# Filtering the sum and the difference of two channel tiles in an attention kernel on TensorE

## What is computed

```python
# x: (16, 256, 32, 32); theta_w, phi_w: (32, 256); g_w: (128, 256); o_w: (256, 128)
theta = einsum('bchw,kc->bkhw', x, theta_w)           # 32 channels, 1024 positions n
phi   = pool2(einsum('bchw,kc->bkhw', x, phi_w))      # 32 channels, 256 positions m
beta  = softmax(einsum('bnk,bkm->bnm', theta, phi))   # over m
g     = pool2(einsum('bchw,kc->bkhw', x, g_w))        # 128 channels, 256 positions
o     = einsum('bchw,kc->bkhw', einsum('bcm,bnm->bcn', g, beta), o_w)
z     = gamma * o + x
out   = z + einsum('fc,bchw->bfhw', tpl, z)   # tpl: circulant 256 x 256, 27 taps wide
```

## Time and profile before

| | us |
|---|---|
| median of 3 runs | 272.98 (272.94 to 273.77) |
| span of the profiled execution | 271.3 |
| PE busy | 265.4 |
| DVE busy | 245.9 |
| ACT busy | 243.2 |
| POOL busy | 149.6 |

### The profile page before, as it was taken

The page is one execution under the profiler, slowest core; times in us unless marked ns, Lnnn a source line. Parts: engine busy times, 40 slices in busy tenths (PEclk is TensorE's granted clock), DMA queues, the critical chain, the costliest instruction groups (busy, mean ns, idle before and its releaser), DMA issues.

```text
span 271.3 us, 4464 instructions
## 1 busy us (share of the span) xinstructions
PE 265.4 (98%) x1196; PEld 211.8 (78%) x1196; DVE 245.9 (91%) x456; ACT 243.2 (90%) x533; POOL 149.6 (55%) x79
## 2 busy tenths in 40 slices
PE   7999999999999999999999999999999999999994
PEld 3576778888888888888888888888887888888873
DVE  4998999999999999999999999999999999999953
ACT  4999999999999999998999999999999989998772
POOL 1585747574565747546673764667466475745100
PEclk9999999999999999999999999999999999999999
DMA  7978085582847657284673828467283855317044
GB/s 198 270 208 212 23 234 169 175 223 81 193 142 225 180 170 182 88 218 149 203 201 144 180 79 246 157 197 206 98 182 124 234 169 172 77 71 178 1 157 155
DMA packets 17380, 44.57 MB, mean 164 GB/s; under 512 B 2654, under 2 KB 3578, under 8 KB 16122
## 3 DMA queue, kind: packets, MB, share of 16 engines
q1 hardware_dynamic: 16682, 44.00, 56.4%
q10 hardware_dynamic: 688, 0.46, 0.5%
HBM read 17.45 MB, written 16.78 MB: 126 GB/s over the span
## 4 chain that ended last, share of the span: by engine, by line
PE 94%; DVE 2%; DMA 2%; ACT 0%; issue 0%; SPq 0%
PE psY L1009 10%; PE psY L988 8%; PE psY L990 7%; PE psY L989 7%; PE psV L1128 6%; PE psY L1112 6%; PE psY L1128 5%; PE psV L1112 5%; PE psV L988 3%; PE psV L990 3%; PE psV L989 3%; PE psX L1066 3%; PE psV L1096 3%; PE psV L1133 3%; PE psZ L1066 3%; PE psY L1118 3%
## 5 line engine op out<-in xcount | busy, mean ns | idle before, releaser
L457 POOL TENSOR_TENSOR prob_lo<-prob,prob_hi 128x1024 fp32r<-128x1024 f32 x30 | 72.1, 2404 | 59.7 <-ACT prob L537 32.5
L450 POOL TENSOR_TENSOR x_lo<-x_raw,x_hi 128x1024 fp32r<-128x1024 f32 x30 | 72.0, 2399 | 35.5 <-ACT x_hi L504 34.0
L504 ACT CAST x_hi<-x_raw 128x1024 fp32r<-128x1024 f32 x30 | 31.5, 1052 | 6.8 <-PE psY L1096 5.2
L526 ACT ACTIVATE psX<-psX,neg_max 128x256 f32<-128x256 f32 x60 | 26.7, 445 | 3.0 <-DVE neg_max L777 3.0
L526 ACT ACTIVATE psZ<-psZ,neg_max 128x256 f32<-128x256 f32 x60 | 27.4, 468 | 0.0
L709 DVE TENSOR_TENSOR thetaphi<-psY,thetaphi_rest 64x512 f32<-64x512 f32 x30 | 20.5, 682 | 3.8 <-ACT thetaphi_rest L508 3.1
L988 PE MATMUL psY<-x_hi,g_hi_w 128*128 128x512 f32 x56 | 22.2, 396 | 0.0
L990 PE MATMUL psY<-x_hi,g_lo_w 128*128 128x512 f32 x56 | 22.0, 393 | 0.0
L989 PE MATMUL psY<-x_lo,g_hi_w 128*128 128x512 f32 x56 | 22.0, 392 | 0.0
L715 DVE TENSOR_TENSOR theta_aug<-thetaphi,theta_aug 32x512 fp32r<-32x512 f32 x30 | 20.5, 683 | 0.9
L702 DVE TENSOR_REDUCE phi_pool<-thetaphi 32x128 f32<-32x512 f32 x30 | 20.2, 674 | 1.0
(11 more groups left out here) (189 smaller groups left out, 766.1 us busy)
## 6 DMA issues: line engine op xcount, KB each, us to landing
x_raw<-x SPq DMA_DIRECT2D x30, 512.0 KB, 5.1
out<-y SPq DMA_DIRECT2D x15, 1024.0 KB, 4.0
x_edge<-x_hi SPq DMA_DIRECT2D x64, 104.0 KB
x_edge<-x_lo SPq DMA_DIRECT2D x32, 104.0 KB
x_raw<-x SPq DMA_DIRECT2D x4, 256.0 KB, 4.5
out<-y SPq DMA_DIRECT2D x3, 256.0 KB, 2.1
band_rev<-ring SPq DMA_DIRECT2D x2, 128.0 KB, 6.9
out<-y ACTq DMA_DIRECT2D x1, 256.0 KB, 2.6
```

What stands on the lines that cost most here:

```text
L450: nc.gpsimd.tensor_tensor(x_lo[:, par, :, cols], x_raw[:, par, :, cols], x_hi[:, par, :, cols].bitcast(F32), ALU.subtract).then_inc(x_lo_r ...
L457: nc.gpsimd.tensor_tensor(prob_lo[:, h], prob[:, h], prob_hi[:, h].bitcast(F32), ALU.subtract).then_inc(prob_lo_ready, 1)
L504: nc.scalar.copy(x_hi[:, par, :, cols], x_raw[:, par, :, cols]).then_inc(x_hi_ready[h], 1)
L526: last = nc.scalar.activation(tiles[:, t, :], tiles[:, t, :], ACT.Exp, bias=neg_max[:, col:col + 1], accum_out=exp_sum[:, col:col + 1])
```

## The change

From image 2 on, the two channel tiles are replaced by their difference (`uv[:, 0]`) and their sum (`uv[:, 1]`). On these the filter is two separate 128x128 matrices, half of A - B and half of A + B, and needs no corner products. The projection weights and the output weights are combined in the same way (`proj_c`, `w2_c`). The outputs of the two tiles are the sum and the difference of the two PSUM results, which `combine` on DVE forms from `y_sum`, a copy of one of them that ACT takes. POOL forms `uv`.

The shifts are made for one half at a time (`shift_half`, `ln_half`), and two small DMAs per half bring them as two rows (high and low) into `theta_aug`; the transposes and `spread_shifts` go. For this, the positions of a score tile are taken with a step of four. The loads of `x_edge` go from image 2 on. The order on all engines is changed, and POOL's waits for `theta_low` go. Images 0 and 1 keep the corner products.

```diff
+            def turn_shifts(i, par, h):
+                for part, ready in enumerate((shift_half_hi_ready, shift_half_parts_ready)):
+                    row = theta_aug[R_SHIFT + part:R_SHIFT + part + 1, par, h * HALF:(h + 1) * HALF]
+                    sp.wait_ge(ready, from_third(2, i, par, h + 1))
+                    sp.dma_start(row.bitcast(F32), shift_cols[:, h, part, :].bitcast(F32)).then_inc(shift_landed[h][part], 16)
+            def load_after_uv(i, par):
+                for h in range(2):
+                    sp.wait_ge(uv_ready[h], from_third(2, i - 1, par, 2))
+                load(i, par)
...
                     image0()
+                    for h in range(2):
+                        sp.wait_ge(x_lo_ready[h], 1)
+                    load(1, 1)
+                    store(0, 0)
+                    load_after_uv(2, 0)
                     return
-                if has_next_but_one(i, par):
+                if has_next(i, par):
                     for h in range(2):
-                        sp.wait_ge(x_lo_ready[h], from_second(1, i, par, 1))
-                    load(i + 1, par)
-                store(*preceding(i, par))
-                if has_next(i, par):
-                    x_edges(*following(i, par))
+                        turn_shifts(*following(i, par), h)
+                    store(i, par)
+                    if has_load(i):
+                        load_after_uv(i + 2, par)
                 else:
...
+            def projection_weights():
+                pool.wait_ge(tp_w_loaded, 16)
+                pool.wait_ge(g_w_loaded, 16)
+                nc.gpsimd.tensor_tensor(proj_c[:, 0], proj_raw[:, 0], proj_raw[:, 1], ALU.subtract).then_inc(proj_c_ready, 1)
+                nc.gpsimd.tensor_tensor(proj_c[:, 1], proj_raw[:, 0], proj_raw[:, 1], ALU.add).then_inc(proj_c_ready, 1)
+                pool.wait_ge(proj_c_ready, 2)
+                nc.gpsimd.tensor_scalar(proj_c[:], proj_c[:], 0.5, None, ALU.mult).then_inc(proj_c_half_ready, 1)
...
+            def form_uv(i, par, h, signs):
+                cols = slice(h * HALF, (h + 1) * HALF)
+                pool.wait_ge(x_loaded[h][par], 16 * (i + par))
+                if not (is_number(i) and (i, par) == (1, 0)):
+                    pool.wait_ge(x_lo_ready[h], from_second(1, i, par, 0))
+                for t in signs:
+                    nc.gpsimd.tensor_tensor(uv[:, t, cols], x_raw[:, par, 0, cols], x_raw[:, par, 1, cols],
+                                            ALU.add if t == 1 else ALU.subtract).then_inc(uv_ready[h], 1)
...
             prob_low(0, 0, 0)
+            form_uv(1, 0, 0, (1, 0))
             prob_low(0, 0, 1)
-            x_low(1, 0, 0)
-            x_low(1, 0, 1)
+            uv_low(1, 0, 0)
+            form_uv(1, 0, 1, (0,))
+            uv_low(1, 0, 1)
...
+                if has_next_but_one(i, par):
+                    form_uv(i + 1, par, 0, (1, 0))
                 if has_next(i, par):
                     for h in range(2):
-                        pool.wait_ge(theta_lo_ready, upto(2, *following(i, par), h + 1))
                         prob_low(i, par, h)
                 if has_next_but_one(i, par):
+                    form_uv(i + 1, par, 1, (1, 0))
                     for h in range(2):
-                        x_low(i + 1, par, h)
+                        uv_low(i + 1, par, h)
...
+                act.wait_ge(uv_ready[h], from_third(2, i, par, 2))
+                act.wait_ge(x_used[h], upto(2, i, par, -2))
+                nc.scalar.copy(x_hi[:, par, :, cols], uv[:, :, cols]).then_inc(x_hi_ready[h], 1)
...
+            def sum_out(i, par, h):
+                act.wait_ge(out_done[h][1], upto(1, i, par, 1))
+                act.wait_ge(out_evacuated[h][0], upto(1, i, par, 0))
...
+                    theta_copy(ni, npar, 0)
...
                     x_high(i + 1, par, 0)
                 o_in_high(i, par, 0)
-                for h in range(2):
-                    exp_sums(ni, npar, h)
-                ln_sums(ni, npar)
+                exp_sums(ni, npar, 0)
+                if is_raw(i):
+                    out_of_psum(i, par, 0, 1)
+                else:
+                    sum_out(i, par, 0)
+                ln_half(ni, npar, 0)
+                exp_sums(ni, npar, 1, 0, 2)
                 if has_next_but_one(i, par):
                     x_high(i + 1, par, 1)
-                for f in (1, 0):
-                    out_of_psum(i, par, 1, f)
+                if is_raw(i):
+                    out_of_psum(i, par, 1, 1)
+                else:
+                    sum_out(i, par, 1)
+                exp_sums(ni, npar, 1, 2, NT)
+                ln_half(ni, npar, 1)
...
+            def shift_half(i, par, h):
                 tiles = slice(h * NT, (h + 1) * NT)
-                rows = theta_aug[R_SHIFT:K_AUG, par, :].rearrange("r (t n) -> r t n", n=P)
-                dve.wait_ge(shift_turned, turned(i, par))
-                row = shift_turned_ps[0:SHIFT_ROWS, :].rearrange("r (o n) -> r o n", o=1).broadcast_to([SHIFT_ROWS, NT, P])
-                nc.vector.tensor_tensor(rows[:, tiles, :], row, own_rows(tiles), ALU.mult).then_inc(shift_rows_ready, 1)
+                high, low = shift_cols[:, h, 0, :], shift_cols[:, h, 1, :]
+                dve.wait_ge(half_ln_sum_ready, from_third(2, i, par, h + 1))
+                nc.vector.tensor_tensor(half_shift_sum_ps[h], neg_max[:, tiles], half_ln_sum_ps[h],
+                                        ALU.subtract).then_inc(shift_half_ready, 1)
+                dve.wait_ge(shift_half_ready, from_third(2, i, par, h + 1))
+                nc.vector.tensor_copy(high, half_shift_sum_ps[h]).then_inc(shift_half_hi_ready, 1)
+                dve.wait_ge(shift_half_hi_ready, from_third(2, i, par, h + 1))
+                nc.vector.tensor_tensor(low, half_shift_sum_ps[h], high.bitcast(F32),
+                                        ALU.subtract).then_inc(shift_half_parts_ready, 1)
...
+            def combine(i, par, h):
+                cols = slice(h * HALF, (h + 1) * HALF)
+                dve.wait_ge(out_evacuated[h][1], upto(1, i, par, 1))
+                dve.wait_ge(out_done[h][0], upto(1, i, par, 1))
+                dve.wait_ge(y_stored[par], 16 * i)
+                upper = nc.vector.tensor_tensor(y[:, par, 0, cols], out_bank(i, par, h, 0), y_sum[:, h], ALU.add)
+                if is_last(i, par):
+                    upper.then_inc(y_upper_ready, 1)
+                nc.vector.tensor_tensor(y[:, par, 1, cols], y_sum[:, h], out_bank(i, par, h, 0),
+                                        ALU.subtract).then_inc(out_evacuated[h][0], 1)
+            def form_u(i, par, h):
+                cols = slice(h * HALF, (h + 1) * HALF)
+                dve.wait_ge(x_loaded[h][par], 16 * (i + par))
+                nc.vector.tensor_tensor(uv[:, 1, cols], x_raw[:, par, 0, cols], x_raw[:, par, 1, cols], ALU.add).then_inc(uv_ready[h], 1)
...
+            def combined_band():
+                dve.wait_ge(band_diagonal_ready, 1)
+                dve.wait_ge(band_rest_ready, 1)
+                nc.vector.tensor_tensor(band_c[:, 0], band[:, 0, 0:P], band[:, 0, P:C], ALU.subtract).then_inc(band_c_ready, 1)
+                nc.vector.tensor_tensor(band_c[:, 1], band[:, 0, 0:P], band[:, 0, P:C], ALU.add).then_inc(band_c_ready, 1)
+                dve.wait_ge(band_c_ready, 2)
+                nc.vector.tensor_scalar(band_hi_c[:], band_c[:], 0.5, None, ALU.mult).then_inc(band_c_hi_ready, 1)
+                dve.wait_ge(band_c_hi_ready, 1)
+                nc.vector.scalar_tensor_tensor(band_lo_c[:], band_c[:], 0.5, band_hi_c[:].bitcast(F32),
+                                               ALU.mult, ALU.subtract).then_inc(band_c_lo_ready, 1)
...
+            form_u(1, 0, 1)
...
-                gT_low(i, par)
+                pool_g(ni, npar, 0)
                 theta_low(ni, npar, 0)
-                pool_g(ni, npar, 0)
                 sum_thetaphi(ni, npar, 1)
                 pool_phi(ni, npar, 1)
                 split_phi(ni, npar)
+                pool_g(ni, npar, 1)
                 theta_low(ni, npar, 1)
-                pool_g(ni, npar, 1)
                 maxima(ni, npar, 0)
                 o_in_low(i, par, 0)
                 maxima(ni, npar, 1)
-                out_of_psum(i, par, 0, 1)
                 o_in_high(i, par, 1)
-                out_of_psum(i, par, 0, 0)
+                shift_half(ni, npar, 0)
                 o_in_low(i, par, 1)
-                shifts(ni, npar)
-                turn_shifts(ni, npar)
-                for h in range(2):
-                    spread_shifts(ni, npar, h)
+                if is_raw(i):
+                    out_of_psum(i, par, 0, 0)
+                    combined_band()
+                    out_of_psum(i, par, 1, 0)
+                    combined_w2()
+                else:
+                    for h in range(2):
+                        combine(i, par, h)
+                shift_half(ni, npar, 1)
             over_images(dve, image)
...
```

(41 more changed lines are left out.)

164 lines of the change are left out of this document (118 added, 46 removed).

## The result

The changed kernel takes **331.2 us** (median of 4 runs, 329.22 to 333.82) against 272.96 for the kernel before: a ratio of 1.213, 95% interval 1.205 to 1.220. It is slower, as forecast, but by 58 us where 29.5 were forecast, and it lies above the range. The page of its profile, to be read beside the earlier trace rows: busy time of each engine, and the granted clock in 40 slices.

A forecast was written before the change was run, and what follows sets the result against it. PE, 98% busy, was taken to bound the kernel before; afterwards a chain through DVE held by POOL. 271.3 + 23.9 (loop) + 4.8 (image 1) + 0.3 (start) + 0.5 (end) = 300.8, plus 1.7: 302.5 us, range 272 to 308.

The forecast's parts named there:

- The hold: A DVE operation meeting a running POOL operation waits for its end; 1.84 us an image, 23.9 us over 13 iterations.
- steps 1 and 2: After ACT, POOL's prob_low(n, 1) ends at S + 8.9; DVE's theta_low(n + 1, 1), held by it, ends at S + 9.3.
- S: The start of sum_thetaphi(n + 1, 0) on DVE, from which the chain of one image is counted.
- Step 3: PE from the start of scores(n + 1, 1) to the end of add_low_attention(n, 0, 0): 0.47 and 20 matmuls, 5.09 us.
- Steps 3 and 4: After PE's 5.09 us, DVE's combine starts 0.30 behind, four at 0.60, then the last shift_half, 0.60, before the next S.
- The start at 0.3: Before the loop: POOL combines weights beside DVE subtractions, bounded at 0 to 1.7 us, taken as 0.3.
- the two first images: The next two images after the loop's first transposes, including the iteration of image 1: +6.6 us forecast.
- The end: Last half waits for a sum_out, two combine operations (+0.95) and its shifts, against four corner matmuls less (-0.92): 0.5 us.
- Held, but in a better order: Rival: theta_low may just beat POOL, but POOL's work and DVE's held operations make 17.0 us an image: 290.8 us; chance 0.18.
- Only the casts are held: Rival: theta_low(n + 1, 1) is not held and ends at S + 7.5, image 16.0 us: 274.6 us; chance 0.13.
- the aim is worth 13 x 0.85: Rival: PE, or ACT at 15.3, sets the pace in the loop; 11 us less there, 264 us; chance 0.14.

The follow-up runs named there:

- The filled gap: Changed kernel with four idle 512-column matmuls on PE between attention_input_low(n, 0) and scores(n+1, 1): 319.7 us.
- the order made certain: Changed kernel with theta_low of half 1 ahead of pool_g on DVE, and POOL waiting for it ahead of prob_low(n, 1): 301.2 us.
- the three edits: Changed kernel with one-PSUM-input theta_low of half 1, neighbouring columns as scores weights (scaled exponentials), and old weights without combining operations: 285.4 us.

## Why the prediction was right in kind and wrong in size

- **The hold** (POOL against DVE, steps 1 and 2) is right, and for its reason. Counted from S in the image at 141.65: POOL ends at S + 8.5 (8.9 forecast), `theta_low` asks at S + 6.97 (6.8 to 6.9) and ends at S + 9.04 (9.3). The sentence that any DVE operation that meets a running POOL operation waits for its end is too wide, though: `sum_thetaphi` of half 1, with one input in PSUM, began inside the POOL operation of 149.12 in the kernel before and took 0.68:

```profile
149.61 0.68 DVE L709 TENSOR_TENSOR thetaphi<-psY,thetaphi_rest 64x512 f32<-64x512 f32 x1
```

The Trainium skill ("SBUF — State Buffer", Who interferes with whom) says that a VectorE instruction with two SBUF inputs contends with a GpSimd instruction that reads SBUF, and that one with at most one SBUF input, outside the two-port modes, does not. The runs agree with both halves, 2.07 and 0.68 us.
- **Step 3** failed in one term: the 0.47 of the scores. With weights of step four the group takes 1.06, and the 20 matmuls 4.64 as counted. It was put down at the present price because the trace had no such load, without an upper bound; an unknown cost needs both. Steps 3 and 4 come to 5.70, 0.38, 2.40 and 0.50, and the image to 18.07 against 17.84. That it comes so near is in part luck: the 0.61 that step 3 lacks is offset by 0.36 too much in step 2 and the wait behind it.
- **The clock has no term in the sum.** This is the step that failed: "PE and ACT then idle" was costed as idle time alone. In seven of twelve images the gap is followed by a stretch at 1.2 GHz, 1.4 us each, 9.8 in all. The filled gap shows it (-11.5). It is the largest single piece of the 28.7 us above the forecast, but not the only one: 7.0 are the start, 3.5 the two first images, 3.7 the steady images at full clock, 2.8 the end, and 2.0 that the median stands above the profiled execution (329.22). Without the clock's 9.8 the time, 321, would still lie above the range.
- **The start at 0.3** and the two first images are undersized: 7.3 and 10.1 measured for 0.3 and 6.6. The estimate had taken 0.3 of a bound of 1.7 for the start and left out the two DVE operations that POOL holds there, `w_lo` (2.26 us for 0.47) and `form_u` (2.78, where an operation of its size takes 0.68 alone). The rows of the start assign 7.2 of the 7.3: 1.5 ahead of the transposes of image 0, 4.0 of waits more than before, 1.7 of lower clock. It is not the combined weights: the start stays without them. Without `form_u` it is 3.1 us shorter, and the next image takes them back. 4 us of the two first images are the combined weights.
- **The end**, 3.3 for 0.5: the shift DMAs, costed at nothing in the steady part, where that held, are waited for here (PE's next weight load comes 3.6 us late), since no matmuls of a next image lie ahead.
- **The rivals.** "Held, but in a better order" was worked out at 290.8; the order made certain gives 301.2. "Only the casts are held" is refuted by `theta_low` at 2.06 to 2.52 us in every image of the loop. That the aim is worth 13 x 0.85 was too much: 0.49 an image.

Open: what sets the 0.65 us between an image of the three edits (16.21) and one of the kernel before without its corners (15.56); POOL's operations made longer by DVE's are a candidate, not tried.

## What to carry to other kernels

A wait that looks idle in a profile may be what keeps two engines apart: before it is removed, look for the two operations that would meet, and which is first by how much. When the forecast puts a gap into a busy TensorE, cost what follows the gap, not the gap alone. And an unknown cost on the critical path (an operand read with another step) needs an upper bound, however small it looks in an image.

## What the chip showed that was not expected

- Who comes second loses, unequally: the 0.68 us of `theta_low` become 2.1 to 2.9 behind a `prob_low` of POOL, and once 3.6; POOL's 2.40 become 2.7 to 2.9 behind DVE. The end of the first POOL operation need not free DVE: `w_lo` stayed held through three in a row, 4.79 us where the kernel before takes 0.47.
- A gap of 1.0 us, once an image, was followed by the lower clock in 7 of 12 images and never when filled. Of two images with the same gap (0.98 and 1.04 us) one had the drop, and the runs don't show why that one. The length of the gap doesn't decide it alone: with neighbouring columns as weights the gaps were 1.4 to 1.9 us long and only 4 of 12 images had the drop, and in the kernel before without POOL's waits 11 of the 12 images had a gap of 0.9 us and none of them a drop.
- Weights of step four (16 bytes), by their loads in the kernel after, minimum, median and maximum; the minimum is that of neighbouring columns, from image 1:

```profile
L1203 PEld LDWEIGHTS psZ<-phi_aug,theta_aug x60: 188/329/334, 29.1 to 302.6; 96*128 96x128 f32 x60
```

The Trainium skill ("SBUF — State Buffer", Door 1: The DMA port swizzle, in its note on cachelines of 16 bytes) says that each access that crosses to a new line pays a penalty, and also that one can stride for free over four elements in fp32. With a step of four every element lies in a line of its own. The runs agree with the first sentence and not with the second: 329 for 188 ns.
